# Key units of an attention block: halves swapped by ScalarE in PSUM, one product over two banks, low parts on GpSimd

## What is computed

```python
x = x + xattn(layernorm(x), ctx, ctx, mask)     # 32 query heads, 8 key/value heads, key size 128
x = x + ffn(layernorm(x))                       # silu(x w1) * (x w2), times w3; weights quantised to NF4 and back

def xattn(query, key, value, mask):
    q, k, v = query @ Wq, key @ Wk, value @ Wv
    q, k = apply_rope(q), apply_rope(k)
    logits = 30 * tanh(q . k * 0.0884 / 30)
    return softmax(where(mask, logits, -1e30)) @ v @ Wo

def rotate_half(x):
    x1, x2 = split(x, 2, axis=-1)
    return concatenate((-x2, x1), axis=-1)

def apply_rope(x):
    return x * cos(phase) + rotate_half(x) * sin(phase)
```

## Time and profile before

| | |
|---|---|
| median of 3 runs | 856.96 us |
| the profiled execution | 855.72 us |
| its span, first to last instruction | 853.9 us |
| TensorE busy | 803.7 us, 94% of the span |
| VectorE busy | 684.7 us, 80% |
| ScalarE busy | 465.5 us, 55% |
| GpSimd busy | 497.8 us, 58% |
| mean granted clock of TensorE | 0.982 |

### The profile page before, as it was taken

How to read it: one execution, slowest core, us unless ns; L and a number is a source line. 1 busy time by engine, 2 the same in 40 slices (tenths; PEclk the granted TensorE clock), 3 DMA queues, 4 the chain that set the end, 5 groups by cost and what they waited for, 6 DMA issues and landing times.

```text
span 853.9 us, 10691 instructions
## 1 busy us (share of the span) xinstructions
PE 803.7 (94%) x3806; PEld 644.9 (76%) x3806; DVE 684.7 (80%) x745; ACT 465.5 (55%) x571; POOL 497.8 (58%) x270
## 2 busy tenths in 40 slices
PE   6798997999999999999999999998879999995998
PEld 4677885777788778877787778776668788884886
DVE  3876862589989899989989889889858999999512
ACT  5014752665665765665666656656325686866410
POOL 2545154776985986978977978967200344544100
PEclk9999998999999999999999999999999999997999
DMA  9676646432343433442533533412301121302112
GB/s 330 192 196 185 188 102 188 133 99 75 109 132 75 125 116 87 124 120 71 167 87 77 157 83 96 132 38 72 108 0 50 50 93 50 117 26 59 55 35 99
DMA packets 63541, 91.76 MB, mean 107 GB/s; under 512 B 6784, under 2 KB 30464, under 8 KB 63488
## 3 DMA queue, kind: packets, MB, share of 16 engines
q1 hardware_dynamic: 62304, 88.25, 35.7%
q10 hardware_dynamic: 1184, 2.82, 0.9%
HBM read 51.00 MB, written 19.07 MB: 82 GB/s over the span
## 4 chain that ended last, share of the span: by engine, by line
PE 81%; DVE 11%; issue 3%; DMA 2%; POOL 1%; ACT 1%; SPq 1%; DVEq 0%; POOLq 0%
PE bank L508 7%; PE bank L510 7%; PE bank L509 7%; PE bank L524 7%; PE bank L526 6%; PE bank L525 6%; PE avp L598 6%; PE bank L570 6%; PE bank L490 5%; PE bank L492 5%; PE bank L491 5%; PE trp L497 4%; DVE nfv L927 2%; PE bank L699 2%; PE bank L700 2%
## 5 line engine op out<-in xcount | busy, mean ns | idle before, releaser
L1247 POOL TENSOR_TENSOR eb<-eb,maskf 128x512 f32<-128x512 f32 x64 | 100.8, 1575 | 60.6 <-ACT eb L801 60.6
L799 ACT ACTIVATE eb<-bank 128x512 f32<-128x512 f32 x64 | 38.2, 597 | 177.6 <-PE bank L570 177.6
L1190 POOL TENSOR_TENSOR qT<-cs_loop,sw 128x512 f32<-128x512 f32 x57 | 101.9, 1787 | 34.8 <-DMA sw<-cs_loop 34.5
L508 PE MATMUL bank<-xh,wqh 128*128 128x512 f32 x256 | 106.5, 416 | 1.2 <-POOL wql L1181 1.2
L524 PE MATMUL bank<-woh,ath 128*128 128x512 f32 x256 | 107.6, 420 | 0.0
L526 PE MATMUL bank<-woh,atl 128*128 128x512 f32 x256 | 101.5, 396 | 0.0
L510 PE MATMUL bank<-xh,wql 128*128 128x512 f32 x256 | 101.5, 396 | 0.0
L525 PE MATMUL bank<-wol,ath 128*128 128x512 f32 x256 | 101.2, 395 | 0.0
L509 PE MATMUL bank<-xl,wqh 128*128 128x512 f32 x256 | 101.2, 395 | 0.0
L927 DVE SCALAR_TENSOR_TENSOR nfv<-nfq,nfv 128x1408 f32<-128x1408 uint8 x42 | 85.5, 2037 | 0.7
L935 DVE TENSOR_TENSOR cs_loop<-bank,csq 128x1024 f32<-128x1024 f32 x57 | 69.1, 1213 | 18.8 <-PE bank L510 18.8
(11 more groups left out here) (150 smaller groups left out, 1983.7 us busy)
## 6 DMA issues: line engine op xcount, KB each, us to landing
sw<-cs_loop SPq DMA_DIRECT2D x114, 128.0 KB, 2.3
stage<-wq_pieces SPq DMA_DIRECT2D x32, 256.0 KB, 3.0
stage<-wo_pieces SPq DMA_DIRECT2D x32, 256.0 KB, 2.8
stage<-dq_scratch SPq DMA_DIRECT2D x32, 256.0 KB, 3.6
sw<-cs_start SPq DMA_DIRECT2D x46, 128.0 KB, 2.3
ks_scratch<-qT SPq DMA_DIRECT2D x16, 256.0 KB, 2.5
vs_scratch<-vst SPq DMA_DIRECT2D x16, 256.0 KB, 3.2
kcur<-ks_scratch SPq DMA_DIRECT2D x16, 256.0 KB, 2.9
```

The source lines that it names most:

```text
L508: nc.tensor.matmul(o, wqh[:, g, k, :], xh[:, k, cs], start=k == 0, stop=False)
L1190: nc.gpsimd.tensor_tensor(dst, products(ru, slot)[:, 0, :], sw[:, slot, :], ALU.add).then_inc(roped, 1)
```

## The change

Two PSUM tensors of two banks each now serve the key units in turn: prjs (the two banks that prj names one by one) and avp. TensorE writes a key unit into the first bank of the pair. ScalarE copies partitions 64 to 127 of it to partitions 0 to 63 of the second bank and the other way about (`key_swap`). VectorE multiplies both banks with the cosines and sines in one operation (`key_parts`), and GpSimd subtracts the second product from the first (`key_rope`), since the sign of the sines belongs to the half before the swap. The swap DMAs of the key units go; the query units keep theirs.

FIRST_POOL gets all lows from 8 to 19: low 9 to 15 stand behind the sums of units 0 to 6, low 16 to 19 behind those of units 11 to 14. VectorE makes lows 5 and 7 ahead of its first product, and no more in the key stage. ScalarE makes highs 0 to 8, then one `key_swap` for each unit with the highs 9 to 21 between them; the DMAs of the tokens and of the first chunk to quantise are issued at other places of its order. SP issues pieces 16 to 22 one per unit. The mask matmul stands behind unit 2 instead of 7, and the mask tables behind product 3 instead of 8; the statistics are divided otherwise, three behind each of products 5 and 6.

```diff
--- before.py
+++ after.py
@@ -141,10 +141,12 @@
         dq3 = nc.dram_tensor("dq3_scratch", (128, NFW), f32, kind="Internal").ap()
 
 
-        bank = [ctx.enter_context(nc.psum_tensor(f"bank{i}", [128, 512], f32)) for i in range(5)]
+        prjs = ctx.enter_context(nc.psum_tensor("prjs", [128, 2, 512], f32))
+        bank = [ctx.enter_context(nc.psum_tensor(f"bank{i}", [128, 512], f32)) for i in range(3)]
         avp = ctx.enter_context(nc.psum_tensor("avp", [128, 2, 512], f32))
         trp = ctx.enter_context(nc.psum_tensor("trp", [128, 512], f32))
-        prj, prj2, lgp = [bank[0], bank[1]], [bank[2], bank[3]], bank[4]
+        prj, prj2, lgp = [prjs[:, 0, :], prjs[:, 1, :]], [bank[0], bank[1]], bank[2]
+        key_pair = [prjs, avp]
         trg = [trp, lgp]
 
 
@@ -172,7 +174,7 @@
         wt_done, wt_hi, wt_lo = sem("wt_done"), sem("wt_hi"), sem("wt_lo")
         gate_done, silu_done, h_done, h_hi, h_lo = (sem("gate_done"), sem("silu_done"), sem("h_done"), sem("h_hi"),
                                                     sem("h_lo"))
-        mask_step = sem("mask_step")
+        mask_step, key_swapped = sem("mask_step"), sem("key_swapped")
         down_done, final_done, stored = sem("down_done"), sem("final_done"), sem("stored")
         block = ctx.enter_context(nc.Block())
 
@@ -190,7 +192,7 @@
 
         NK = 16
         WQ0, WO0 = 24, 28
-        FIRST_POOL = (0, 3, 6, 8, 10, 16, 18, 20, 22, 24, 26)
+        FIRST_POOL = (0, 3, 6, *range(8, 20), 20, 22, 24, 26)
         NF_BUF = [nfa, nfv, nfx]
 
         def nf_bufs(c):
@@ -355,10 +357,9 @@
             for n in range(5, 16):
                 first_piece(n)
             for u in range(NK):
-                swap(u, u % 2)
                 if u > 0:
                     k_store(u - 1)
-                for n in {6: (16, 17), 7: (18, 19), 14: (20,), 15: (21, 22)}.get(u, ()):
+                for n in {4: (16,), 5: (17,), 6: (18,), 7: (19,), 13: (20,), 14: (21,), 15: (22,)}.get(u, ()):
                     first_piece(n)
             k_store(NK - 1)
             for n in range(23, 28):
@@ -542,7 +543,7 @@
                     split(pe, 5 + u if half == 0 else 16)
                 wait(pe, cs_done, u - 1)
                 cs = slice(half * 512, (half + 1) * 512)
-                wh, wl, o = wch[kv // 4][:, kv % 4, :], wcl[kv // 4][:, kv % 4, :], prj[u % 2][:, :]
+                wh, wl, o = wch[kv // 4][:, kv % 4, :], wcl[kv // 4][:, kv % 4, :], key_pair[u % 2][:, 0, :]
                 for k in range(KT):
                     if u == 0:
                         split(pe, k + 2)
@@ -551,7 +552,7 @@
                     nc.tensor.matmul(o, wh[:, ks], ctl[:, k, cs], start=False, stop=False)
                     last = nc.tensor.matmul(o, wl[:, ks], cth[:, k, cs], start=False, stop=k == KT - 1)
                 last.then_inc(proj_done, 1)
-                if u == 7:
+                if u == 2:
 
                     pe.wait_ge(masks, 1)
                     pe.wait_ge(consts, 1)
@@ -759,7 +760,7 @@
 
                 src, arrived, value = source(n)
                 if 16 <= n < WQ0:
-                    act.wait_ge(proj_done, 12 if n < 20 else 16)
+                    act.wait_ge(proj_done, n - 7)
                 act.wait_ge(arrived, value)
                 nc.scalar.activation(parts(n)[0], src, ACT.Copy).then_inc(piece_hi, 1)
 
@@ -769,15 +770,25 @@
                 nc.scalar.activation(xh[:, :, i * 128:(i + 1) * 128],
                                      trp[:, :].rearrange("p (k t) -> p k t", k=KT), ACT.Copy).then_inc(xt_hi, 1)
 
-            for n in range(16):
+            def key_swap(u):
+
+                act.wait_ge(proj_done, u + 1)
+                pair = key_pair[u % 2]
+                nc.scalar.activation(pair[0:64, 1, :], pair[64:128, 0, :], ACT.Copy)
+                nc.scalar.activation(pair[64:128, 1, :], pair[0:64, 0, :], ACT.Copy).then_inc(key_swapped, 1)
+
+            for n in range(9):
                 first_hi(n)
-                if n == 9:
-                    act.dma_start(y[:, :, :], x_d.rearrange("b s d -> s b d")).then_inc(x_in, 16)
-            act.dma_start(nfv[:, :], nf_d[:, 0:CH]).then_inc(nf_in, 16)
-            for u in range(10, NK):
-                first_token_hi(u - 10)
-                if u >= 12:
-                    first_hi(u + 4)
+            act.dma_start(y[:, :, :], x_d.rearrange("b s d -> s b d")).then_inc(x_in, 16)
+            for u in range(NK):
+                key_swap(u)
+                for n in {0: (9, 10), 1: (11, 12), 2: (13,), 3: (14,), 4: (15,)}.get(u, ()):
+                    first_hi(n)
+                if u == 4:
+                    act.dma_start(nfv[:, :], nf_d[:, 0:CH]).then_inc(nf_in, 16)
+                if u >= 10:
+                    first_token_hi(u - 10)
+                    first_hi(u + 6)
             act.wait_ge(consts, 3)
             for v in range(16):
                 act.wait_ge(vproj_done, v + 1)
@@ -785,7 +796,7 @@
                 nc.scalar.activation(vst[:, v % 4, :], prj2[v % 2][:, :], ACT.Copy).then_inc(v_copied, 1)
                 if v < 2:
                     first_token_hi(6 + v)
-                for n in range(20 + 2 * v, 22 + 2 * v) if v < 4 else ():
+                for n in {0: (22, 23), 1: (24,), 2: (25, 26), 3: (27,)}.get(v, ()):
                     first_hi(n)
                 for i in nf_values(v + 1):
                     nf_above_bound(0, i)
@@ -938,6 +949,16 @@
                     both.rearrange("p c (o t) -> p c o t", o=1).to_broadcast([128, 2, 4, S]), ALU.mult)\
                     .then_inc(cs_done, 1)
 
+            def key_parts(u):
+
+                dve.wait_ge(key_swapped, u + 1)
+                wait(dve, roped, u - 1)
+                nc.vector.tensor_tensor(
+                    products(u, u % 2).rearrange("p c (b t) -> p c b t", b=4),
+                    key_pair[u % 2][:, :, :].rearrange("p c (b t) -> p c b t", b=4),
+                    tab[:, 0:2, :].rearrange("p c (o t) -> p c o t", o=1).to_broadcast([128, 2, 4, S]), ALU.mult)\
+                    .then_inc(cs_done, 1)
+
             nc.vector.memset(ones[:, :], 1.0).then_inc(consts, 1)
             nc.vector.memset(vcur[:, :, :], 1.0).then_inc(consts, 1)
             for i in range(15):
@@ -1013,27 +1034,26 @@
                     dve.wait_ge(xt_done, i + 1)
                     normalise(i + 2, nrm)
 
+            for n in (5, 7):
+                first_low(n)
             dve.wait_ge(tab_in, 16)
             for u in range(NK):
-                rope_parts(u, u % 2, tab[:, 0:2, :])
-                for n in {0: (5,), 1: (7,), 2: (9, 12), 3: (11, 13), 4: (14,), 5: (15,)}.get(u, ()):
-                    first_low(n)
+                key_parts(u)
+                if u == 3:
+                    mask_tables()
                 if u == 5:
                     dve.wait_ge(x_in, 16)
-                    for b in range(4):
+                if u in (5, 6):
+                    for b in range(3 * u - 15, 3 * u - 12):
                         nc.vector.bn_stats(stat[:, b, :], y[:, b, :])
-                if u == 6:
-                    ln_moments(0, range(B), 4)
                 if u == 7:
+                    ln_moments(0, range(B), 6)
+                if u == 8:
                     ln_rstd(0, range(B))
                     normalise(0, nrm)
                     normalise(1, nrm)
-                if u == 8:
-                    mask_tables()
                 if u >= 10:
                     token(u - 10)
-                if u in (13, 14):
-                    first_low(2 * u - 9)
             nf_prepare(0)
             for v in range(16):
                 if v < 2:
@@ -1186,8 +1206,14 @@
             def rope(ru, slot, dst):
 
                 pool.wait_ge(cs_done, ru + 1)
-                pool.wait_ge(swapped[slot], 32 * (ru // 2 + 1))
+                pool.wait_ge(swapped[slot], 32 * ((ru - NK) // 2 + 1))
                 nc.gpsimd.tensor_tensor(dst, products(ru, slot)[:, 0, :], sw[:, slot, :], ALU.add).then_inc(roped, 1)
+
+            def key_rope(u, dst):
+
+                pool.wait_ge(cs_done, u + 1)
+                part = products(u, u % 2)
+                nc.gpsimd.tensor_tensor(dst, part[:, 0, :], part[:, 1, :], ALU.subtract).then_inc(roped, 1)
 
             def first_low(n):
 
@@ -1216,16 +1242,18 @@
                 pool.wait_ge(nf_acc, 15 * c + 15)
                 nf_blocks(nf_bufs(c)[1], nfm[:, c % 2, :]).then_inc(nf_scaled, 1)
 
-            for n in (0, 3, 6):
+            for n in (0, 3, 6, 8):
                 first_low(n)
             for u in range(NK):
                 if u >= 8:
                     pool.wait_ge(k_out[u - 8], 16)
-                rope(u, u % 2, qT[:, u % 8 // 4, u % 4, :])
-                for n in {0: (8,), 2: (10,), 12: (16,), 13: (18,)}.get(u, ()):
-                    first_low(n)
-                if u == 5:
+                key_rope(u, qT[:, u % 8 // 4, u % 4, :])
+                if u < 7:
+                    first_low(u + 9)
```

(3 more changed lines are left out.)

## The result

The changed kernel takes 849.02 us in the median (848.94 to 849.15, 4 runs), the one before 857.05 beside it; the ratio is 0.9904, with a 95% interval of 0.9887 to 0.9921. That is 8.0 us less, where 8.7 were forecast. In a second set of runs the same kernel gave 850.02 against 857.04, ratio 0.9916 (0.9895 to 0.9937). The profiled executions took 855.72 before and 849.01 after.

A forecast was written before the change was run, and what follows sets the result against it. The key stage was taken as bound by a ring through the DMA swap. Values 7.2 us sooner plus 1.5 in the first value unit make 8.7, subtracted from the 856.96 median: 848.3 us, range 846.0 to 852.6.

The forecast's parts named there:

- The bound: Key stage: a ring of unit, product, DMA swap, sum, next product; the new one needs 5.51 us per two units.
- The start: Key units 1 and 2: unit 1 starts without a wait at 11.15 instead of 13.40, unit 2 at 13.9 instead of 17.82.
- Rival (c): Key stage: slower ScalarE copies, 2.3 us a pair, lose about 6 of 8.7 us, giving 854; chance 12%.
- The mask tables: VectorE behind product 3: five operations of some 0.28 us, with the product 2.6, still within a unit.
- Low 15: GpSimd behind sum 6: done at 33.4, so unit 8 starts at 33.5 after TensorE idles 2.6 us.
- Rival (d): Key stage: GpSimd becomes the bound; low 15 comes late, 853 to 866 us; chance 5%.
- The clock ahead of unit 8: Unit 8: the clock drops behind the 2.6 us wait, so it takes 4.42 us instead of 2.82, 1.6 more.
- rival (a): Unit 8: the clock stays up behind the 2.6 us wait, 1.6 us more gained, 846.7; chance 12%.
- Behind unit 8 and the values: Unit 11 starts at 44.1, the values at 61.9, 7.2 us sooner; full clock in the first value unit gives 1.5.
- rival (b): The clock also drops ahead of the values, or the key stage's tail waits longer: 1.5 us back, 849.8; chance 20%.
- What is late next: Value stage and the weight-piece wait at 145.39 follow TensorE, so the whole gain of 8.7 us reaches the end.
- Rival (e): Later stages: a wait that doesn't follow TensorE swallows the gain, 856 to 857 us; chance 4%.

## Why the prediction was right, step by step

- **The bound (right).** The ring over the DMA swap held the key stage: lows 5 and 7 moved alone gave nothing, the whole order without the copies cost 6 us, and one more copy in the new ring cost 2 to 3 us. The new ring takes 5.59 us for two units, forecast 5.51.
- **The start (right, 0.3 to 0.5 off).** Units 1 and 2 start at 11.42 and 14.36, against 11.15 and 13.9. Unit 0 had a wait of 0.17 for a context piece; the pair of copies is 1.15 and not 1.09. Rival (c), slower copies, did not come.
- **The mask tables (mis-sized).** "Five operations of some 0.28 … still within a unit": they took 3.1 us, because two of them read two SBUF operands beside GpSimd. The prediction used the collision for GpSimd's length only, and forgot that its new lows would stretch VectorE's small operations. The Trainium skill's rule on the shared SBUF interfaces ("GPSIMD Engine Reference", "Specifications") speaks of both; 1.08 and 1.38 beside 0.28 agree with it. Units 6 and 7 started at 27.06 and 29.88, 1.9 and 2.0 us late (unit 5 had been 0.5 late), and unit 8 at 35.12, not at 33.5. With the tables moved it was 33.32.
- **Low 15 (right).** The wait ahead of unit 8 is 2.35 us, forecast 2.6, with GpSimd's low as its releaser; GpSimd's sums and lows are 1.26 to 1.35 there. Rival (d) did not come.
- **The clock ahead of unit 8 (wrong in this profile, and wrong as a rule).** A drop was counted, 1.6 us; the profile of the change shows none. Unit 9 started at 37.99, forecast 37.9: the missed 1.6 and the mask tables cancelled. The step read a bound between 1.80 and 2.02 out of three waits; the same kernel in another execution did drop, and the lower row fell too: behind 1.81 us at the same unit 9 (42.46) the clock went down within the unit in the kernel with lows 5 and 7 moved. So the condition of rival (a) came in this profile, and its 846.7 did not, since the mask tables took as much. That the forecast of unit 9 is met is luck. What was needed there was a chance, not a rule.
- **Behind unit 8 and the values (right).** Unit 11 at 44.59 (43.9 to 44.7 forecast), the values at 62.70 (61.9), the wait ahead of them 1.53 (1.6), with the clock up. So 6.4 us and not 7.2, and 1.5 for the clock as forecast, 7.9 together. Of the missing 0.8, 0.5 stands ahead of unit 11 (44.1 was taken from a range of 43.9 to 44.7, and about 1 us of the small operations there is VectorE held up beside GpSimd), and 0.3 in the four units from 11 to 15, which take 3.29 us each, not 3.2. Of rival (b), the tail's part came by half and the drop did not; 849.02 lies midway between the forecast of 848.3 and its 849.8. And the 1.5 is the price in one execution of before: with lows 5 and 7 moved, the same wait of 2.02 us was followed by the full clock, so how much of it is in the medians is not shown.
- **What is late next (right).** The value stage and the wait behind it followed whole: 8.0 at SP's issue, 8.0 in the median. Rival (e) did not come. Not seen: the value stage had no margin left for more, as the kernels with low 15 on VectorE and with the value lows two units earlier show.

## What to carry to other kernels

When a swap of partition halves by DMA stands in a ring, two ScalarE copies within PSUM and a product over two banks shorten the ring; check then whether it is still longer than the matmuls, since idle time of the copying engine is not slack. Work moved to GpSimd must be costed twice: in its own length, and in that of VectorE's operations beside it, those with two SBUF operands and small ones between SBUF tiles too. And a wait of TensorE of 1.8 us or more should be priced with a chance of the slow clock, not with a threshold read from a few waits.

## What the runs showed of the hardware

The clock behind waits of 1.8 to 3.6 us is not settled by the kernel. Behind 2.35 us it stayed at 1.00 in one execution of the change and fell to 0.50 in another; behind 3.57 and 2.75 us two executions of one kernel gave opposite answers at both places; behind the 2.02 us ahead of the values it fell in the kernel before and stayed up with lows 5 and 7 moved (69.07 to 72.28). Behind the 1.80 us ahead of unit 9 it stayed up in the kernel before; behind 1.81 us at the same place, with lows 5 and 7 moved, it fell, as the lengths of the matmuls show:

```profile
42.46 0.47 PE L550 MATMUL bank<-cth,wch 128*128 128x512 f32 x1 [1.81 <-DVE cs_start L935]
...
43.92 0.62 PE L550 MATMUL bank<-cth,wch 128*128 128x512 f32 x1
```

Over the waits ahead of key and value units in all 14 profiles, between 8 and 84 us: all 21 of 1.02 to 1.53 us were followed by the full clock, 9 of the 15 of 1.80 to 3.57 us and all 4 of 4.26 to 6.01 us by a lower one in the unit behind. A drop made that unit 1.2 to 2.5 us longer, which is as large as most single edits here, except at 42.46, where another wait stood behind the unit and hid it. Executions of one kernel lie 2 to 7 us apart in all sets but the first (before: 854.95 to 861.21), and no profile shows whether the drops alone make that up. What settles the clock was not found.

A 64x512 ScalarE copy from PSUM to PSUM takes 0.57 us, one of the same shape and source to SBUF 0.58 (L779 of the kernel with one more copy), the 128x512 copy from PSUM to SBUF 0.60. Two of the first in a row start 0.58 apart, without the overlap of 0.11 that the earlier trace rows show, since they read PSUM from different start partitions. The Trainium skill, "ScalarE: Activation LUTs", section "Step-by-step: what each stage is for", says that ScalarE is faster to PSUM, and 0.57 against 0.58 agrees, by 0.01 us only; its section "What ACT_TABLE_LOAD costs" says that ACTIVATEs in a row overlap by about 0.09, and here these two do not.

GpSimd holds up more of VectorE than operations with two SBUF operands: the 128x8 TENSOR_SCALAR at 40.91, with one tensor in, took 1.16 us beside a sum and takes 0.17 without one. Products that read PSUM were not held up (1.22 with a sum or low beside them and without).
